# A router's logits from the probabilities by token: GpSimd multiplies, VectorE sums, in place of six small matrix products

## The reference, cut to what matters

```python
nx = _layer_norm(x, ln_gamma, ln_beta)
q = nx @ Wq;  k = prototype_bank @ Wk;  v = prototype_bank @ Wv      # prototype_bank: 154 x 256
weights = softmax(einsum('bth,bph->btp', q, k) * H ** (-0.5))
evidence = einsum('btp,bph->bth', weights, v)
combined = concatenate([nx, evidence, anchor], axis=-1)
router_logits = combined @ router_W + router_b                        # 3 experts
router_probs = softmax(router_logits)
h = silu(einsum('btc,ecr->bter', combined, e_w1) + e_b1)
expert_out = einsum('bter,erh->bteh', h, e_w2) + e_b2
routed = sum(expert_out * router_probs[..., None], axis=-2)
g = sigmoid(silu(combined @ gate_w1 + gate_b1) @ gate_w2 + gate_b2)
x = x + g * (routed @ out_w + out_b)
```

## Time and profile before

| | |
|---|---|
| median of 3 runs | 434.74 us (433.83 to 435.14) |
| the profiled execution's own time | 433.71 us |
| its span, first to last instruction | 431.8 us |
| TensorE products, busy | 415.3 us, 96% |
| TensorE weight loads, busy | 378.9 us, 88% |
| VectorE, busy | 291.0 us, 67% |
| ScalarE, busy | 219.5 us, 51% |
| GpSimd, busy | 173.5 us, 40% |
| TensorE's granted clock, mean | 1.000 |

### The profile page before, as it was taken

How to read it: one execution, slowest core, us unless ns; L and a number is a source line. 1 busy time by engine, 2 the same in 40 slices (tenths; PEclk the granted TensorE clock), 3 DMA queues, 4 the chain that set the end, 5 groups by cost and what they waited for, 6 DMA issues and landing times.

```text
span 431.8 us, 9528 instructions
## 1 busy us (share of the span) xinstructions
PE 415.3 (96%) x3581; PEld 378.9 (88%) x3581; DVE 291.0 (67%) x740; ACT 219.5 (51%) x487; POOL 173.5 (40%) x175
## 2 busy tenths in 40 slices
PE   7989999999999999999999999999999899988996
PEld 6668999999999899988998899889988898877875
DVE  2685476682766497738864896488657865783787
ACT  2777643335428633773357436743673257326271
POOL 6345573253462256125532544255425731341010
PEclk9999999999999999999999999999999999999999
DMA  8777001640200130105000300040003011300301
GB/s 297 230 281 312 25 3 26 177 94 13 62 3 3 38 87 27 28 18 173 8 4 2 108 18 5 0 100 2 5 1 99 2 34 37 92 3 28 73 2 50
DMA packets 16981, 27.67 MB, mean 64 GB/s; under 512 B 3816, under 2 KB 9256, under 8 KB 16808
## 3 DMA queue, kind: packets, MB, share of 16 engines
q1 hardware_dynamic: 16808, 27.06, 21.4%
q10 hardware_dynamic: 128, 0.01, 0.0%
HBM read 15.80 MB, written 2.10 MB: 41 GB/s over the span
## 4 chain that ended last, share of the span: by engine, by line
PE 87%; DVE 7%; ACT 3%; issue 2%; SPq 0%; DMA 0%; ACTq 0%
PE hidden_banks L1725 9%; PE hidden_banks L1726 9%; PE hidden_banks L1727 9%; PE score_banks L1732 7%; PE token_bank L1725 6%; PE token_bank L1726 6%; PE token_bank L1727 6%; PE score_banks L2097 5%; PE score_banks L2067 4%; PE value_bank L2120 3%; PE hidden_banks L1950 3%; PE value_bank L2123 3%; PE value_bank L1732 3%; PE head_bank L1732 2%; DVE head_maxima L1484 1%
## 5 line engine op out<-in xcount | busy, mean ns | idle before, releaser
L1659 POOL TENSOR_TENSOR hidden_low<-hidden,hidden_high 128x512 fp32r<-128x512 f32 x56 | 72.9, 1301 | 144.1 <-ACT hidden_high L1083 140.0
L1725 PE MATMUL hidden_banks<-normed_high,hidden_w_high 128*128 128x256 f32 x224 | 64.2, 287 | 0.8 <-issue 0.8
L1484 DVE TENSOR_REDUCE head_maxima<-score_banks 128x2 f32<-128x308 f32 x128 | 53.8, 471 | 14.5 <-PE score_banks L2067 12.6
L1726 PE MATMUL hidden_banks<-normed_high,hidden_w_low 128*128 128x256 f32 x224 | 62.5, 279 | 0.0
L1727 PE MATMUL hidden_banks<-normed_low,hidden_w_high 128*128 128x256 f32 x224 | 62.4, 279 | 0.0
L1145 ACT ACTIVATE exp_ring<-score_banks 128x512 f32<-128x512 f32 x96 | 52.5, 600 | 18.3 <-PE score_banks L2097 17.4
L1083 ACT CAST hidden_high<-hidden 128x512 fp32r<-128x512 f32 x56 | 34.8, 621 | 47.2 <-DVE hidden L1401 45.4
L1075 ACT ACTIVATE hidden<-hidden_banks 128x512 f32<-128x512 f32 x56 | 33.3, 595 | 45.7 <-PE hidden_banks L1950 44.1
L1725 PE MATMUL token_bank<-expert_out_high,hidden_high 128*128 128x256 f32 x192 | 55.6, 290 | 0.1
L1726 PE MATMUL token_bank<-expert_out_high,hidden_low 128*128 128x256 f32 x192 | 53.4, 278 | 0.0
L1727 PE MATMUL token_bank<-expert_out_low,hidden_high 128*128 128x256 f32 x192 | 53.4, 278 | 0.0
(11 more groups left out here) (299 smaller groups left out, 1080.1 us busy)
## 6 DMA issues: line engine op xcount, KB each, us to landing
unit_weights<-units SPq DMA_DIRECT2D x7, 768.0 KB, 6.3
query_stack<-queries_high SPq DMA_DIRECT2D x56, 64.0 KB, 2.0
tokens<-x SPq DMA_DIRECT2D x8, 256.0 KB, 3.6
query_stack<-queries_low SPq DMA_DIRECT2D x28, 64.0 KB, 2.0
w_slice<-units SPq DMA_DIRECT2D x7, 256.0 KB, 3.0
out<-tokens SPq DMA_DIRECT2D x7, 256.0 KB, 2.4
w_T<-folds SPq DMA_DIRECT2D x6, 256.0 KB, 5.9
pair_keys<-keys_high SPq DMA_DIRECT2D x16, 77.0 KB
```

Of the source, the lines that this page charges most:

```text
L1484: v.tensor_reduce(MX[:, s, first:first + step + 1:step], S[:, ring_of[key][0], 0:2 * CTX].rearrange("p (j n) -> p j n", j=2), AX.X, ALU.ma ...
L1659: nc.gpsimd.tensor_tensor(SL[:, ring(t, u), :], TB[:, ring(t, u), :], raw(SH[:, ring(t, u), :]), ALU.subtract).then_inc(gpsimd_h, 1)
L1725: mm(out_, lh, rh, start=start, stop=False, skip_group_check=skip)
L1726: mm(out_, ll, rh, start=False, stop=False, skip_group_check=skip)
```

## The change

The context's share of the logits is computed by token instead of through the turned probabilities. In `fold` six full-precision products with a broadcast router column as the loaded side give, in every partition, the three rows (one for each expert) of 154 values "context value times router column" (`router_rows`). GpSimd multiplies the probabilities of a tile by each row (`rmul`, three instructions of 128x2x154) and adds the upper 77 of the terms to the lower 77 (`rsum`); VectorE sums the 77 and adds the result to the logits. The rows hold one batch at a time: for the second batch TensorE makes them again in head_bank ahead of tile 3's hidden units (`rows`), and VectorE copies them.

The terms lie at the place of x_hat and the normed tokens. So x_hat of the next tile waits for the logits of this one, while the transposes of x_hat no longer wait for them. Some tiles in SBUF change place (tail rows beside the values, the sums), and the table gets slots for the new steps; the logits of tile 7 are moved forward, and the memsets `zero` behind a low half.

```diff
-    "ln": -5.7, ... "prob": 9.1, "route": 12.3, "logit": 14.4, "res": 17.4,
+    "ln": -5.7, ... "prob": 9.1, "route": 12.3, "rmul": 10, "rsum": 11, "rows": 13.4, "logit": 14.4, "res": 17.4,
...
+        TERMS = put("router_terms", [P, NSUB, EXPERTS, CTX], offset=xhat_at)
+        VR = put("router_rows", [P, EXPERTS, CTX])
...
             def logit(key):          # VectorE
                 t = key[1]
-                dve.wait_ge(tensor_logit, upto(tensor_logit, key, "l"))
                 dve.wait_ge(vector_att, upto(vector_att, ("att", t), "t"))
-                parts_of = H[:, 0:8 * NSUB].rearrange("p (s i e) -> p i s e", i=2, e=4)
-                v.tensor_tensor(LG[:, :, :], LG[:, :, :], parts_of[:, 1, :, 0:EXPERTS], ALU.add)...
+                dve.wait_ge(gpsimd_rsum, upto(gpsimd_rsum, ("rsum", t), "s"))
+                v.tensor_reduce(RTS[:, :, :], TERMS[:, :, :, 0:CTX // 2], AX.X, ALU.add)...
                 dve.wait_ge(vector_results, results.n)
-                v.tensor_tensor(LG[:, :, :], LG[:, :, :], parts_of[:, 0, :, 0:EXPERTS], ALU.add).then_inc(vector_logit, 1)
+                v.tensor_tensor(LG[:, :, :], LG[:, :, :], RTS[:, :, :], ALU.add).then_inc(vector_logit, 1)
...
             def norm(key):           # GpSimd: x_hat
                 if t:
                     pool.wait_ge(gpsimd_prob, upto(gpsimd_prob, ("prob", t - 1), "p"))
+                    pool.wait_ge(vector_logit, upto(vector_logit, ("logit", t - 1), "l"))
...
+            def router_mul(key):     # GpSimd
+                t = key[1]
+                pool.wait_ge(gpsimd_prob, upto(gpsimd_prob, ("prob", t), "p"))
+                pool.wait_ge(gpsimd_low, upto(gpsimd_low, ("low", t), "n"))
+                pool.wait_ge(scalar_norm, upto(scalar_norm, ("norm", t), "n1"))
...
+                for e in range(EXPERTS):
+                    last = nc.gpsimd.tensor_tensor(TERMS[:, :, e, :], PB[:, :, 0:CTX], VR[:, e, :].unsqueeze(1).to_broadcast([P, NSUB, CTX]),
+                                                   ALU.mult)
+                last.then_inc(gpsimd_rmul, 1)
+
+            def router_sum(key):
+                t = key[1]
+                pool.wait_ge(gpsimd_rmul, upto(gpsimd_rmul, ("rmul", t), "m"))
+                half = CTX // 2
+                nc.gpsimd.tensor_tensor(TERMS[:, :, :, 0:half], TERMS[:, :, :, 0:half], TERMS[:, :, :, half:CTX], ALU.add).then_inc(gpsimd_rsum, 1)
...
+            def router_rows(bank, b):    # TensorE, in fold for the first batch, in rows_again for the second
+                for e in range(EXPERTS):
+                    last = plain(bank[:, CTX * e:CTX * e + CTX],
+                                 [(RW[:, KC + k, e:e + 1].to_broadcast([P, P]), VL[b][:, k, 0:CTX]) for k in range(KC)])
+                return last
...
             def norm(key):           # TensorE: transposes of x_hat
                 if t:
-                    pe.wait_ge(vector_logit, upto(vector_logit, ("logit", t - 1), "l"))
+                    pe.wait_ge(vector_route, upto(vector_route, ("route", t - 1), "dl"))
...
-            def logit(key):          # TensorE: the six products of a tile
-                pe.wait_ge(vector_route, upto(vector_route, ("route", t), "dl"))
-                for s in range(NSUB):
-                    c = slice(P * s, P * s + P)
-                    mm(H[:, 8 * s:8 * s + 8], PTh[:, t % 2, c], VRC[:, b, 0, :], start=(s == 0), ...)
-                    mm(H[:, 8 * s:8 * s + 4], PTl[:, t % 2, c], VRC[:, b, 0, 0:4], start=False, ...)
-                    last = mm(H[:, 8 * s:8 * s + 4], PTD[0:STACK, t % 2, c], VRC[0:STACK, b, 1, 0:4], start=False, ...)
```

More of the change, by code:

```diff
@@ L151 @@
         "prob": ["p"],
-        "logit": ["l"],
+        "rows": ["r"],
         "z": ["z"],
@@ L210 @@
         "route": ["pl", "dl"],
+        "rows": ["c"],
         "logit": ["l", "s", "prob"],
@@ L279 @@
     "dup": (37.2, 49.2), "za": -0.4, "step": 1.99, "z": 0.38, "h": 1.5, "p": 3.3, "again": -6.4, "vw": -38.8,
-    "ln": -5.7, "norm": 1.6, "low": 6.6, "att": 7.9, "prob": 9.1, "route": 12.3, "logit": 14.4, "res": 17.4,
+    "ln": -5.7, "norm": 1.6, "low": 6.6, "att": 7.9, "prob": 9.1, "route": 12.3, "rmul": 10, "rsum": 11, "rows": 13.4, "logit": 14.4, "res": 17.4,
     "qn": 18.4, "shift": 18.5, "xhat": 19.3, "qx": 19.54, "qlow": 20.1, "query": 20.7,
@@ L294 @@
     1: {
-        "logit": 15.4, "z": 0.62, "ln": 0.2,
+        "z": 0.62, "ln": 0.2,
     },
@@ L355, in schedule @@
         place(SETUP["vt"][u], ("vt", u))
-    for name in ("norm", "low", "att", "prob", "route", "logit"):
+    for name in ("norm", "low", "att", "prob", "rmul", "rsum", "route", "logit"):
         place(SETUP[name], (name, 0))
@@ L387, in schedule @@
         if t:
-            for name in ("ln", "norm", "low", "att", "prob", "route", "logit"):
+            for name in ("ln", "norm", "low", "att", "prob", "rmul", "rsum", "route", "logit"):
                 place(at - LOOP + plan(t, name), (name, t))
@@ L415, in schedule @@
             place(at + plan(t, "reload"), ("reload", t))
+    place(FIRST + LOOP * (AGAIN - 1) + PLAN["rows"], ("rows", 0))
     return table
@@ L551, in build @@
         WS = put("w_slice", [P, 2, KC, UCOLS])
-        VTT1 = put("values_T1", [P, KC, P])
-        LT = [put(f"tail_rows{b}", [P, KC, 32]) for b in range(BATCH)]
-        SCW2, KTT, VTT0, OB, used0 = run(keys_at, [
+        VL1 = put("values_T1", [P, KC, P + 32])
+        SCW2, KTT, VL0, OB, used0 = run(keys_at, [
             ("query_score_w_raw", [P, KC, D], F32), ("keys_T", [P, KC, 160], F32),
-            ("values_T0", [P, KC, P], F32),
+            ("values_T0", [P, KC, P + 32], F32),
             ("out_b_row", [P, D], F32)])
@@ L566, in build @@
         SCW = [part[:, KC * 160:].rearrange("p (k n) -> p k n", k=KC) for part in (FW0, FW1)] + [SCW2]
-        VTT = (VTT0, VTT1)
+        VL = (VL0, VL1)
+        VTT = [part[:, :, 0:P] for part in VL]
+        LT = [part[:, :, P:P + 32] for part in VL]
+        at[0] += 256
         hidden_at = at[0]
@@ L949, in context_v @@
                 columns = context_bank(b)[:, 0:320].rearrange("p (k n) -> p k n", k=KC)
-                nc.scalar.copy(VTT[b][:, :, :], columns[:, :, 0:P]).then_inc(scalar_cv, 1)
+                nc.scalar.copy(VTT[b], columns[:, :, 0:P]).then_inc(scalar_cv, 1)
                 nc.scalar.copy(LT[b][:, :, 0:TAIL], columns[:, :, P:CTX]).then_inc(scalar_cv, 1)
@@ L1559, in _ @@
                      "vw": context_w, "vt": context_tail, "w2": w2, "cb": bias_out, "mod": mod, "bq": query_bias, "keyn": keyn, "key": pair_keys, "ln": ln,
-                     "att": att, "prob": prob, "route": route, "logit": logit, "z": hidden, "init": init, "evac": evac,
+                     "att": att, "prob": prob, "route": route, "rows": rows_copy, "logit": logit, "z": hidden, "init": init, "evac": evac,
                      "res": res, "qn": qn, "shift": shift, "qlow": qlow, "query": query, "most": most, "row": row, "dup": dup, "outl": outs_low, "sums": sums,
```

81 lines of the change are left out of this document (43 added, 38 removed).

## The result

The changed kernel took 452.75 us (median of 4 runs, 451.44 to 453.44), the kernel before 434.41 beside it: ratio 1.042 (95% interval 1.040 to 1.044), slower by 18.3 us. The forecast was 447, with 441 to 453 as its range; the direction is right, and the time lies at the upper end, outside the 442 to 450 that the forecast had for itself.

A forecast was written before the change was run, and what follows sets the result against it. TensorE's queue was taken to bound the kernel: 433.71 − 3.5 (TensorE's side) + 3.2 (multiplications) + 13.0 (new wait) = 446.4, on the median's level 447.4, predicted 447. Range 441 to 453; the forecast's own 442 to 450 had chance 0.60.

The forecast's parts named there:

- What bounds the kernel: Whole span: TensorE's own queue sets the time, with 87% of the chain of waits and the clock at full speed.
- The new wait: Boundaries 1 to 6: x_hat of the next tile waits for this tile's logits, a chain of 4.67 us; +13.0 us.
- The multiplications: GpSimd's three products ahead of the fifth hidden unit's low half delay TensorE's product `p` in four tiles; +3.2 us.
- TensorE's side: TensorE's queue: logit products removed −5.6, set-up products +1.05, fold −0.68, second batch's rows +1.73; sum −3.5 us.
- the 1.05 for its products: Set-up: six full-precision products of 1.73 us replace small products of 0.68 us on TensorE; +1.05 us.
- Contention: First rival: GpSimd's products and x_hat run slower beside VectorE's two-input steps; 452.5 us, chance 0.15.
- The logits did move forward with TensorE: Second rival claimed the opposite: VectorE's queue holds the logits, five boundaries cost 0.70 us more each; 450.9 us, chance 0.12.
- The stalls were not absorbed: Third rival claimed the opposite: no stalls at the boundaries, only TensorE's queue counts; 431.2 us, not slower, chance 0.07.

## Why the prediction was right, and where it was short

- **What bounds the kernel.** Right: with TensorE's queue full, each wait that stands in it shows in the time, and next to nothing is made good later: with the wait alone in the old kernel the boundaries and the falls of the clock cost 13.2 us, and the last `p` is 12.6 late.
- **The new wait.** Right in mechanism, place and size: 13.0 forecast, 13.4 seen; alone in the old kernel 9.6 forecast, 9.6 measured (11.0 in its one trace); taken away (with the falls of the clock) 14.2 back. The reduction was taken as 0.64 and took 0.61 to 0.63; x_hat as 2.40 to its follower, which it took at five boundaries; at boundary 1 it took 2.95.
- **The multiplications.** Right in mechanism, short in size: 3.2 forecast, 4.9 seen, 5.0 back when moved. The step that was too small is the three products as 2.25 us: they took 2.30 beside tile 2 and 2.47 to 2.61 beside tiles 3 to 7, so that four tiles lost 4.0 and not 3.2. The other is tile 7, counted at nothing, which lost 0.91. Tiles 1 and 4, also counted at nothing, lost 0.09 and −0.07.
- **TensorE's side.** The step that "what is taken out of that queue comes back" failed in part: the removal alone is worth 3.7 us and not 5.6. The set-up cost more than the 1.05 for its products: from the fold's first product to the first `p` are 28.65 us now (9.69 to 38.34) and were 27.05 (10.32 to 37.37), since the multiplications push GpSimd's weight splits (26.43 to 29.01) beside VectorE's steps for the second bias (0.48 to 1.39) and TensorE waits 1.02 us for VectorE:

```profile
27.91 1.39 DVE L1295 SCALAR_TENSOR_TENSOR second_bias<-second_bias_high,constants,second_bias_full 128x256 fp32r<-128x256 f32 x1
...
29.90 1.10 PE L1766 MATMUL score_banks<-unit_weights,values_T 128*128 128x256 f32 x4 [1.02 <-DVE context_w_low L1198]
```

- **The clock**, 2.9 us in this profile, stands in no step. The granted clock was read as "full speed in every slice", and not asked what it does once the engine idles. It is the largest part of the 5.7 us between the 12.7 of the forecast's sum and the 18.4 seen in the traces; the fifth unit is 1.7, TensorE's side and the rest 0.7, the boundaries 0.4.
- **The rivals.** Contention gave 452.5, nearly the measured time, but by luck and not by its terms: it wanted x_hat dear at six boundaries (it was at one) and products at 2.82. And it is this rival that had set the upper end of the range: the forecast's own 442 to 450 was missed, so that the time lies inside 441 to 453 is luck too. The logits did move forward with TensorE. The stalls were not absorbed.
- **What stays open.** Why the clock fell behind boundary 4 in one execution and not in another, after the same wait of 1.0 us, and why not behind boundary 2 in the changed kernel's trace, after 2.15 us, when it fell there in the next after 2.14; the 0.31 us at tile 4; and how much of the 18.3 us between the medians the clock is, since 2.9 is one execution's and the kernel before has falls in some of its own.

## What to carry to other kernels

When a new tile is laid over an old one, the price is the last reader of the new tile: trace the wait through the in-order queue of the engine that writes there, up to the bounding engine, and compare the chain with the time that this engine has queued meanwhile. Here the last read could be made a step of its own as early as its inputs allow; that and one slot number turned 18 us slower into no change, and with the addition moved too into 1 us faster. Moving work from TensorE to GpSimd and VectorE also moved inputs from PSUM to SBUF, and an addition of 0.14 us then took 1.20 beside a GpSimd step. Look for such meetings, but price them where they delay the wait that ends last: beside tile 6 VectorE came 0.60 us late and GpSimd's low half hid it.

## What the runs showed of the hardware

- A wait of TensorE of 1.0 to 2.5 us was at some places followed by 3.4 us, once 6.8, at a granted clock of 0.50, in which products begin every 0.21 us instead of 0.12: up to 1.5 us more than the wait itself. At others, after as long a wait, the clock stayed at 1.00 (boundary 2 in the changed kernel after 2.15 us; tile 7 in the kernel before after 2.19). With products in the gap it did not fall at any of the six boundaries of the one trace.
- A VectorE addition of 128x6 with both inputs in SBUF took 1.20 us beside a GpSimd step of 1.29 that had begun 0.11 us earlier, and 0.14 to 0.17 without one.
- Three GpSimd products of 128x2x154 took 2.30 us from start to follower with no VectorE step of two SBUF inputs beside them and 2.47 to 2.61 with one, which took 0.83 to 1.18 us instead of 0.48.
